# Graph layer with counted tiles: one-hot tiles handed over in runs of two or three, and tallies added two column groups late

## The chip, the cores and the metric

The kernel runs on one core of one Trainium2 chip. The metric is device time in microseconds (us) of one execution, the median of several runs; lower is better.

## What is computed

```python
def gnn(node_feats, src, dst, ...):
    neigh = segment_sum(node_feats[src], dst, num_segments=n)
    h = (1.0 + eps) * node_feats + neigh
    h = relu(h @ W1 + b1) @ W2 + b2
    return batch_norm(h) * gamma + beta

x = x + gnn(layernorm(x), src, dst, ...)          # 12500 nodes of 256 features, 200000 edges sorted by dst
x = x + ffn(layernorm(x), ...)                    # 8 experts, top 1, capacity 1.25
```

The edges are sorted by their target and are denser at low targets (the targets are 12500 times the square of a uniform number). The change lies wholly in the first step, `segment_sum(node_feats[src], dst)`.

## The kernel before

The program has four stages, one behind the other: `stage_norm` (layer norm, the table of rows in DRAM, and a plan of the edges), `stage_edges` (the segment sum and the two small matrix products), `stage_route` and `stage_experts`. Only `stage_edges` is touched.

An edge tile is 128 edges. The edges with the densest targets, 328 tiles (`HT`), are *counted*; all others, 1240 tiles, are *gathered*.

**Gathered tiles** come in 155 groups of 8 (`GT`), taken in iterations `n` of three groups `r` (`RG` = 3 buffers `got`). GpSimd (POOL) issues 8 indirect DMAs for each group (line 791). It may fill a buffer again once TensorE has finished the sums of the group that was in it (`s_sum`). VectorE makes 8 one-hot tiles `hot` for a group (L1070, L1076), TensorE multiplies them with the gathered rows, 16 matmuls (L879), and VectorE adds the result of the group before to the nodes (L1062).

**Counted tiles** are never gathered. For each, VectorE writes a wide one-hot of the source block (490 columns, L1113) and a one-hot of the target (128 columns, L1115) into a ring `tall` of `OR` = 6 tiles. TensorE multiplies the two (L907) into one of `BANKS` = 4 PSUM banks `tally`. Tiles that share a window of targets form a *column group* (`GROUP_OF`): 4 tiles for the first 96, 2 tiles up to tile 168, one tile each for the other 160, 220 column groups in all. When a column group is complete, VectorE adds its bank to `counts` (L1126, in `count(group)`). There are five units. After the tiles of a unit, `fold` adds what is still in the banks. Then for four iterations (mixed iterations) TensorE multiplies `counts` with pieces of the table (L917), which SP loads.

The order of work is written out and is the same on every engine, for each (n, r): the counted tiles of (n, r), then the gathered group, then pieces, then in some places a *quad*, the two matrix products of 512 nodes (L928, L936, L942 on TensorE; about 25 us in which TensorE does nothing else). 64 of the (n, r) have counted tiles, 3 to 12 each. Six quads stand directly ahead of an (n, r) with counted tiles: those at (13,1), (21,2), (28,2), (30,2), (36,0) and (38,0). Behind them come 4, 4, 3, 3, 5 and 3 tiles, all of one-tile column groups.

The handshake is one count per tile: TensorE waits for `s_tall >= t + 1` and signals `s_tile`; VectorE waits for `s_tile` before it writes a place of the ring again. With three column groups of delay, `counted(t)` at the start of column group g calls `count(g - 3)`.

Of the kernel before, what the change touches and what calls it, by code (L numbers as in the profile page):

```python
# [10 lines left out]
ALU = mybir.AluOpType  # L11
# [7 lines left out]
P = 128  # L19
# [18 lines left out]
RG = 3  # L38
# [4 lines left out]
GROUPS = ((96, 4), (168, 2), (328, 1))  # L43
NU = len(UNIT_TILES)
TW = 5
FIRST = tuple(sum(sum(tiles) for tiles in UNIT_TILES[:u]) for u in range(NU + 1))
HT = FIRST[NU]
PHASES = []
GROUP_OF = []
# [10 lines left out]
NIT = -(-NG // RG)  # L60
# [5 lines left out]
KEY = HI * TW  # L66
OH = KEY + P
# [19 lines left out]
TILES, MIXED = {}, {}  # L87
# [9 lines left out]
SPREAD = {n + 1: u for n, (u, i) in MIXED.items() if i == MIX - 1}  # L97
# [2 lines left out]
      18: (44, 1), 19: (45, 2), 1: (46, 1), 20: (47, 0), 21: (48, 1), 22: (49, 2), 23: (51, 0)}  # L100
ORDER = sorted(AT, key=lambda q: AT[q]) + [NQ - 1]
assert sorted(ORDER) == list(range(NQ)) and PIECES * RG * MIX * XK == HI - HI % XK


def closed_before(group):
# [196 lines left out]
def flat32(tensor):  # L302
    return tensor[:, :, :].rearrange("p a b -> p (a b)")
# [336 lines left out]
def stage_edges(nc, norm, halves, table, rows_of, targets, buf, ident, nodes, plan, stats, w1f, w2f, W1, W2, W1s, W2s, b1s,  # L640
                b2s):
    with ExitStack() as ctx:
# [3 lines left out]
        def psum(name, shape, dt):  # L646
            return ctx.enter_context(nc.psum_tensor(name, shape, dt))

        def sem(name):
            return ctx.enter_context(nc.semaphore(name))  # L650

        OR = 6
        BANKS = 4
# [3 lines left out]
        COUNT_ZEROS = -(-HI * CW // (2 * ZR * ROW))  # L657
        OWN = 17
        part = flat32(w1f).bitcast(F16)[:, 0:2 * XK * 2 * D].rearrange("p (r k d) -> p r k d", r=2, k=XK)
        tall = flat32(w2f).bitcast(F16)[:, 0:OR * OH].rearrange("p (r c) -> p r c", r=OR)  # L660
# [19 lines left out]
        tally = psum("e_tally", [P, BANKS, 2 * D], F32)  # L680
# [13 lines left out]
        s_tall, s_tile, s_count, s_fold, s_blank = (  # L694
            sem("e_tall_s"), sem("e_tile"), sem("e_count"), sem("e_fold"), sem("e_blank"))
# [22 lines left out]
        def quads_at(n, r):  # L718
            return [q for q in ORDER[:-1] if AT[q] == (n, r)]

        def tiles_at(n, r):

            tiles = TILES.get(n, ())
            parts = (0, 0, 1, 2) if n in SPREAD or n == 0 else (0, 1, 2, 3)
            return tiles[len(tiles) * parts[r] // parts[RG]:len(tiles) * parts[r + 1] // parts[RG]]

        def piece_number(u, i, r, c):
            return u * (MIX * RG * PIECES + 1) + (i * RG + r) * PIECES + c

# [4 lines left out]
        def pieces_at(n, r):  # L734
            if n not in MIXED:
                return []
            u, i = MIXED[n]
            last = i == MIX - 1 and r == RG - 1
            return [piece_number(u, i, r, c) for c in range(PIECES + last)]

        with nc.Block() as block:
# [102 lines left out]
            def _(pe):  # L844
# [5 lines left out]
                with pe.If(general_rounds(pe) > 0):  # L850
                    with pe.Fori(0, general_rounds(pe)) as g:
                        first, end_ = block_range(pe, pe.value_load(ranges_of[0:1, at(g)], min_val=0, max_val=1 << 14))
                        pe.wait_ge(s_pgot, g * (16 * PT) + 16 * PT)
                        with pe.Fori(first, end_):
# [3 lines left out]
                            for t in range(PT):  # L858
                                for half in range(2):
                                    ins = nc.tensor.matmul(sums[:, 0, 0:D], hot[:, 0, t, :],  # L860
                                                           some_rows[:, t, half * D:(half + 1) * D],
                                                           start=(t == 0 and half == 0), stop=(t == PT - 1 and half == 1))
# [2 lines left out]
                        pe.sem_inc(s_pfree, 1)  # L865
                    pe.reg_mov(turn, 1)

                pe.sem_inc(s_tile, OR)
                pe.sem_inc(s_used, 2)
                left = pe.alloc_register("left")  # L870

                def gathered_once(number):
                    r, place = number % RG, (number + 1) % 2
                    pe.wait_ge(s_got[r], (number // RG + 1) * (16 * GT))
                    pe.wait_ge(s_hot, number + 1)
                    pe.wait_ge(s_add, number + 1)
                    for t in range(GT):
                        for half in range(2):
                            ins = nc.tensor.matmul(sums[:, place, 0:D], hot[:, place, t, :],  # L879
                                                   got[:, r, t, half * D:(half + 1) * D],  # L880
                                                   start=(t == 0 and half == 0), stop=(t == GT - 1 and half == 1))
                    ins.then_inc(s_sum, 1)
# [17 lines left out]
                    pe.wait_ge(s_sum, turn)  # L900
                    pe.sem_inc(s_free, 1)

                def count(t):

                    group = GROUP_OF[t]
                    pe.wait_ge(s_tall, t + 1)
                    nc.tensor.matmul(tally[:, group % BANKS, 0:KEY], tall[:, t % OR, KEY:OH], tall[:, t % OR, 0:KEY],  # L907
                                     start=(t == GROUP_OF.index(group)), stop=(group not in GROUP_OF[t + 1:])
                                     ).then_inc(s_tile, 1)

                def piece(number):
                    k0, width = piece_columns(number)
# [34 lines left out]
                pe.wait_ge(s_w, 32)  # L947
                for n in range(NIT):
                    for r in range(RG):
                        for t in tiles_at(n, r):  # L950
                            count(t)
                        if n * RG + r < SINGLE:
                            gathered_once(n * RG + r)
                        elif n * RG + r < NG:
                            gathered(n, r)
                        for number in pieces_at(n, r):
                            piece(number)
                        for q in quads_at(n, r):
                            quad(q)
# [48 lines left out]
            def _(dve):  # L1008
# [99 lines left out]
                    ins.then_inc(s_spread, 1)  # L1108
                    dve.wait_ge(s_spread, flushed[0])

                def one_hots(t):
                    dve.wait_ge(s_tile, t + 1)
                    nc.vector.tensor_scalar(tall[:, t % OR, 0:KEY], plan.iota[:, :], plan.key[:, t:t + 1], None,  # L1113
                                            ALU.is_equal)
                    nc.vector.tensor_scalar(tall[:, t % OR, KEY:OH], plan.iota[:, 0:P], plan.low[:, t:t + 1], None,  # L1115
                                            ALU.is_equal).then_inc(s_tall, 1)

                def count(group):

                    last_tile = len(GROUP_OF) - 1 - GROUP_OF[::-1].index(group)  # L1120
                    column = dve.value_load(plan.cols[0:1, group:group + 1], min_val=0, max_val=P - 1)
                    dve.wait_ge(s_tile, OR + last_tile + 1)
                    if group > 0:
                        dve.wait_ge(s_count, group)
                    place = counts[:, :, bass.ds(column, TW)]
                    nc.vector.tensor_tensor(place, place, tally[:, group % BANKS, 0:KEY].rearrange("p (k d) -> p k d", d=TW),  # L1126
                                            ALU.add).then_inc(s_count, 1)

                def counted(t):

                    one_hots(t)
                    unit = max(u for u in range(NU) if FIRST[u] <= t)
                    if t == FIRST[unit] or GROUP_OF[t - 1] != GROUP_OF[t]:
                        group = GROUP_OF[t] - (BANKS - 1)
                        if group == GROUP_OF[FIRST[unit]]:
                            dve.wait_ge(s_blank, (unit + 1) * COUNT_ZEROS)
                        if group >= GROUP_OF[FIRST[unit]]:
                            count(group)

                def fold(u):  # L1140
                    for group in range(GROUP_OF[FIRST[u + 1] - 1] - (BANKS - 2), GROUP_OF[FIRST[u + 1] - 1] + 1):
                        count(group)
                    dve.wait_ge(s_count, GROUP_OF[FIRST[u + 1] - 1] + 1)
                    wide = counts[:, :, 0:CW - P]
                    nc.vector.tensor_tensor(wide, wide, counts[:, :, P:CW], ALU.add).then_inc(s_fold, 1)
# [19 lines left out]
                def quad(q, turns):  # L1165
                    k = ORDER.index(q)
                    if k > 0:
                        measure(ORDER[k - 1])
                    dve.wait_ge(s_add, turns)
                    nc.vector.tensor_scalar(hrow.rearrange("p t d -> p (t d)"), nodes[:, q, :], 1.0, None,  # L1170
                                            ALU.mult).then_inc(s_hrow, 1)

                for n in range(NIT):
                    if n in MIXED and MIXED[n][1] == 0:
                        fold(MIXED[n][0])
                    for r in range(RG):
                        for t in tiles_at(n, r):
                            counted(t)
                        if n * RG + r < SINGLE:
                            gathered_once(n * RG + r)  # L1180
                        elif n * RG + r < NG:
                            gathered(n, r)
                        if n in SPREAD and r == 0:
                            spread(SPREAD[n], n * RG + 2 if n * RG < SINGLE else turn)
                        for q in quads_at(n, r):
                            quad(q, n * RG + r + 2 if n * RG < SINGLE else turn)
# [820 lines left out]
```

## Time and profile before

| | |
|---|---|
| median of 3 runs | 3169.5 us |
| the runs | 3169.5, 3172.03, 3138.97 us |
| span of the profiled execution | 3175.1 us |
| busy in it: PE, PEld, DVE, ACT, POOL | 1826, 1098, 1443, 695, 1710 us |
| stage with the edges | from about 138 us to about 2290 us |
| counted tiles | from 141 us to 1700 us, in five stretches |

PE is TensorE's matmuls, PEld its weight loads, DVE VectorE, ACT ScalarE, POOL GpSimd; SP issues plain DMAs. The profile gives a span and no separate device time for the profiled execution; its span lies 5.6 us (0.2%) above the median. An idle time in a row is the time in which the engine had nothing to do just before the instruction, and the name behind the arrow is what ended it; "issue" means that the profile shows nothing it waited for, "remote" that the signal came from something that the profile does not place.

### The profile page before, as it was taken

The numbers are of one execution on the slowest core, as the hardware profiler recorded it, in microseconds if no ns is written. First come the engines' busy times: TensorE is split into PE (matmuls) and PEld (weight loads), VectorE is DVE, ScalarE is ACT, GpSimd is POOL, SyncE is SP. The second block draws the span as 40 slices with busy tenths as digits, with TensorE's granted clock in tenths as the row PEclk, the third lists the DMA queues.
The fourth block names the chain that finished last, engine by engine and source line by source line (L and its number), as shares of the span: only waits on it lengthen the run. The fifth ranks groups of instructions, "written<-read, shape, count | busy, mean of one in ns | idle before, by whom it ended". The sixth has DMA issues, their size and how long they took to land. (4 is left out here: it accounts for less than half of the span.)

```text
span 3175.1 us, 32785 instructions
## 1 busy us (share of the span) xinstructions
PE 1826.2 (58%) x9046; PEld 1097.7 (35%) x9047; DVE 1442.5 (45%) x4225; ACT 694.9 (22%) x1116; POOL 1710.4 (54%) x1690
## 2 busy tenths in 40 slices
PE   0154444455545455655554455564568768989995
PEld 0022212222222222322222222232357645566664
DVE  8765511543225422531252112122336557786885
ACT  6600000000010001000100001110046554636642
POOL 0366664655645565555644444445315556767874
PEclk9976667676767677777877777777776688999997
DMA  7533354324633354234423332212246432222220
GB/s 244 188 104 106 116 184 138 106 88 132 197 101 91 115 182 148 87 121 144 152 65 121 120 111 65 67 54 79 54 145 216 131 93 75 71 84 73 79 83 18
DMA packets 201521, 361.08 MB, mean 114 GB/s; under 512 B 62117, under 2 KB 125947, under 8 KB 201334
## 3 DMA queue, kind: packets, MB, share of 16 engines
q0 software_dynamic: 69152, 185.00, 19.3%
q1 hardware_dynamic: 130038, 172.60, 16.8%
q8 instruction: 108, 1.77, 0.2%
q10 hardware_dynamic: 2144, 1.05, 0.1%
q14 instruction: 79, 0.65, 0.1%
HBM read 291.08 MB, written 71.92 MB: 114 GB/s over the span
## 5 line engine op out<-in xcount | busy, mean ns | idle before, releaser
L791 POOL DMA_INDIRECT halves<-table,halves x1240 | 1187.7, 958 | 1011.5 <-issue 367.1
L879 PE MATMUL e_sums<-halves 128*128 128x256 f16 x1920 | 334.7, 346 | 392.8 <-issue 244.1
L1062 DVE SCALAR_TENSOR_TENSOR nodes<-e_sums,above,nodes 128x256 f32 (+1 forms) x161 | 77.3, 480 | 967.0 <-remote 437.4
L879 PEld LDWEIGHTS e_sums<-halves 128*128 128x128 f16 x1920 | 229.6, 122 | 508.3 <-issue 425.7
L936 PE MATMUL e_up<-e_hT,W1s 128*128 128x512 f32 (+1 forms) x400 | 229.8, 734 | 234.9 <-ACT e_hT L985 140.2
L985 ACT ACTIVATE e_hT<-e_up 128x1024 f32<-128x1024 f32 (+1 forms) x25 | 25.2, 1007 | 1524.0 <-remote 1185.3
L1720 POOL TENSOR_TENSOR x_midl<-x_midf,x_midh 128x512 f16<-128x512 f32 x200 | 298.7, 1517 | 104.9 <-ACT x_midh L1854 99.4
L917 PE MATMUL e_tally<-w1f,counts 128*128 128x512 f16 x490 | 165.5, 480 | 281.6 <-DMA w1f<-table 204.9
L1126 DVE TENSOR_TENSOR counts<-counts,e_tally 128x490 f32 x220 | 159.8, 726 | 267.8 <-PE e_tally L907 147.9
L1810 PE MATMUL x_down<-halves,x_midh 128*128 128x256 f16 x1472 | 249.4, 277 | 16.6 <-DVE x_yb L1947 15.0
L1786 PE MATMUL x_up<-x_xTh,halves 128*128 128x512 f16 (+1 forms) x800 | 233.6, 371 | 3.1 <-ACT x_midh L1854 3.1
L936 PEld LDWEIGHTS e_up<-e_hT,W1s 128*128 128x128 f32 x400 | 91.8, 240 | 355.8 <-issue 177.8
L1810 PE MATMUL x_down<-halves,x_midl 128*128 128x256 f16 x736 | 203.9, 277 | 0.0
L907 PE MATMUL e_tally<-w2f 128*128 128x490 f16 x328 | 126.0, 467 | 135.0 <-DVE w2f L1115 76.5
L1076 DVE TENSOR_SCALAR halves<-ring,e_rel 128x128 f16 x960 | 175.9, 273 | 59.0 <-issue 26.4
L942 PE MATMUL e_up<-e_mid,W2s 128*128 128x512 f32 (+1 forms) x400 | 183.8, 614 | 28.2 <-ACT e_mid L988 28.2
L917 PEld LDWEIGHTS e_tally<-w1f,counts 128*128 128x128 f16 x490 | 48.4, 113 | 374.6 <-DMA w1f<-table 235.4
L1734 POOL DMA_INDIRECT out<-x_res,x_nodei x100 | 116.1, 1161 | 87.3 <-issue 66.7
L1324 POOL DMA_INDIRECT slot_rows<-r_row,r_slots x100 | 97.7, 977 | 117.7 <-ACT r_row L1419 49.9
L1810 PEld LDWEIGHTS x_down<-halves,x_midh 128*128 128x128 f16 x1472 | 145.9, 99 | 40.4 <-issue 11.6
L1786 PE MATMUL x_up<-x_xTl,halves 128*128 128x512 f16 (+1 forms) x400 | 148.2, 371 | 0.0
L896 PE MATMUL e_sums<-halves 128*128 128x256 f16 x640 | 91.6, 305 | 89.5 <-DVE nodes L1062 55.6
(208 smaller groups left out, 2752.4 us busy)
## 6 DMA issues: line engine op xcount, KB each, us to landing
w1f<-table SPq DMA_DIRECT2D x120, 512.0 KB
halves<-table,halves POOLq DMA_INDIRECT x1240
slot_rows<-halves SPq DMA_DIRECT2D x64, 268.0 KB
x_row<-slot_rows SPq DMA_DIRECT2D x32, 536.0 KB, 7.4
table<-halves SPq DMA_DIRECT2D x25, 512.0 KB, 2.9
counts<-in_x SPq DMA_DIRECT2D x24, 512.0 KB, 4.5
r_xin<-in_x SPq DMA_DIRECT2D x24, 512.0 KB
out<-r_row SPq DMA_DIRECT2D x24, 512.0 KB
```

What stands on the lines that cost most here:

```text
L791: pool.indirect_dma_start(got[:, r, t, :], None, table.rearrange("p h d -> (p h) d"), bass.IndirectOffsetOnAxis(ap=idx[:, r, t:t + 1], axi ...
L879: ins = nc.tensor.matmul(sums[:, place, 0:D], hot[:, place, t, :], got[:, r, t, half * D:(half + 1) * D], start=(t == 0 and half == 0), st ...
L907: nc.tensor.matmul(tally[:, group % BANKS, 0:KEY], tall[:, t % OR, KEY:OH], tall[:, t % OR, 0:KEY], start=(t == GROUP_OF.index(group)), st ...
L917: ins = nc.tensor.matmul(product, counts[:, k0 + k, 0:P], part[:, number % 2, k, :], start=(k0 + k == 0), stop=(k0 + k == HI - 1))
L936: ins = nc.tensor.matmul(up[:, c % 2, 0:width], W1s[:, j, c * P:(c + 1) * P], hT[:, j, 0:width], start=(j == 0), stop=(j == DK - 1))
L942: ins = nc.tensor.matmul(up[:, c, 0:width], W2s[:, j, c * P:(c + 1) * P], mid[:, j, 0:width], start=(j == 0), stop=(j == H1C - 1))
L1076: ins = nc.vector.tensor_scalar(hot[:, place, t, :], plan.ring[:, ring_at(shift)], rel[:, place, t:t + 1], None, ALU.is_equal)
L1126: nc.vector.tensor_tensor(place, place, tally[:, group % BANKS, 0:KEY].rearrange("p (k d) -> p k d", d=TW), ALU.add).then_inc(s_count, 1)
L1720: nc.gpsimd.tensor_tensor(midl[:, j % 2, c, :], midf[:, c % MB, :], midh[:, j % 2, c, :], ALU.subtract).then_inc(s_mlo, 1)
L1734: pool.indirect_dma_start(out, bass.IndirectOffsetOnAxis(ap=nodei[:, j, t:t + 1], axis=0), res[:, j % RR, t, :], None, bounds_check=bound, ...
L1786: ins = nc.tensor.matmul(up[:, c % MB, 0:tiles * P], w[:, h, k, cols], x[:, j % 2, k, 0:tiles * P], start=(n == 0), stop=(n == len(passes) ...
L1810: ins = nc.tensor.matmul(down[:, t, :], m[:, j % 2, k, rows], w[:, h, k, :], start=(n == 0), stop=(n == len(passes) - 1))
```

## The change

- The tiles of an (n, r) are cut into runs: of three while the first tile is under 168, of two above, with a shorter run at the end where the number doesn't divide. 328 tiles give 149 runs (45 of three, 89 of two, 15 of one).
- VectorE writes all one-hots of a run and signals `s_tall` once; TensorE waits once, does the run's matmuls and signals `s_tile` once. VectorE waits before a run for the run that holds the tile 6 ahead of its last one.
- The tallies of column group g - 2 are added at the start of column group g, where it was g - 3. This happens after all one-hots of the run: `counted(run)` makes the run's one-hots first and then all adds that the run's tiles call for. `fold` is left with two adds where it had three.

```diff
+def runs_at(n, r):
+    tiles, runs = list(tiles_at(n, r)), []
+    while tiles:
+        size = 3 if tiles[0] < GROUPS[1][1 - 1] else 2
+        runs.append(tiles[:size])
+        tiles = tiles[size:]
+    return runs
+
+RUN_OF = [k for k, run in enumerate(run for n in range(NIT) for r in range(RG) for run in runs_at(n, r)) for _ in run]
...
-                pe.sem_inc(s_tile, OR)
...
-                def count(t):
-
-                    group = GROUP_OF[t]
-                    pe.wait_ge(s_tall, t + 1)
-                    nc.tensor.matmul(tally[:, group % BANKS, 0:KEY], tall[:, t % OR, KEY:OH], tall[:, t % OR, 0:KEY],
-                                     start=(t == GROUP_OF.index(group)), stop=(group not in GROUP_OF[t + 1:])
-                                     ).then_inc(s_tile, 1)
+                def count(run):
+
+                    pe.wait_ge(s_tall, RUN_OF[run[0]] + 1)
+                    for t in run:
+                        group = GROUP_OF[t]
+                        ins = nc.tensor.matmul(tally[:, group % BANKS, 0:KEY], tall[:, t % OR, KEY:OH],
+                                               tall[:, t % OR, 0:KEY], start=(t == GROUP_OF.index(group)),
+                                               stop=(group not in GROUP_OF[t + 1:]))
+                    ins.then_inc(s_tile, 1)
...
-                def one_hots(t):
-                    dve.wait_ge(s_tile, t + 1)
-                    nc.vector.tensor_scalar(tall[:, t % OR, 0:KEY], plan.iota[:, :], plan.key[:, t:t + 1], None,
-                                            ALU.is_equal)
-                    nc.vector.tensor_scalar(tall[:, t % OR, KEY:OH], plan.iota[:, 0:P], plan.low[:, t:t + 1], None,
-                                            ALU.is_equal).then_inc(s_tall, 1)
+                def one_hots(run):
+                    if run[-1] >= OR:
+                        dve.wait_ge(s_tile, RUN_OF[run[-1] - OR] + 1)
+                    for t in run:
+                        nc.vector.tensor_scalar(tall[:, t % OR, 0:KEY], plan.iota[:, :], plan.key[:, t:t + 1], None,
+                                                ALU.is_equal)
+                        ins = nc.vector.tensor_scalar(tall[:, t % OR, KEY:OH], plan.iota[:, 0:P], plan.low[:, t:t + 1],
+                                                      None, ALU.is_equal)
+                    ins.then_inc(s_tall, 1)
...
-                    dve.wait_ge(s_tile, OR + last_tile + 1)
+                    dve.wait_ge(s_tile, RUN_OF[last_tile] + 1)
...
-                def counted(t):
-
-                    one_hots(t)
-                    unit = max(u for u in range(NU) if FIRST[u] <= t)
-                    if t == FIRST[unit] or GROUP_OF[t - 1] != GROUP_OF[t]:
-                        group = GROUP_OF[t] - (BANKS - 1)
...
+                def counted(run):
+
+                    one_hots(run)
+                    unit = max(u for u in range(NU) if FIRST[u] <= run[0])
+                    for t in run:
+                        if t == FIRST[unit] or GROUP_OF[t - 1] != GROUP_OF[t]:
+                            group = GROUP_OF[t] - (BANKS - 2)
...
-                    for group in range(GROUP_OF[FIRST[u + 1] - 1] - (BANKS - 2), GROUP_OF[FIRST[u + 1] - 1] + 1):
+                    for group in range(GROUP_OF[FIRST[u + 1] - 1] - (BANKS - 3), GROUP_OF[FIRST[u + 1] - 1] + 1):
```

## Rows read from the trace of the kernel before

**Rows 1.** Busy time in stretches: all five counting stretches, then the rest.
```profile
138.00:382.00 244.00, 113.52 (x480) 57.43 (x480) 144.80 (x568) 0.00 (x0) 160.12 (x165) 0.70 0.36 109
534.00:741.00 207.00, 96.33 (x378) 50.54 (x377) 103.31 (x353) 11.91 (x20) 124.72 (x130) 0.69 0.37 112
880.00:1074.00 194.00, 94.00 (x345) 47.82 (x343) 85.83 (x285) 16.95 (x27) 101.42 (x108) 0.70 0.32 99
1231.00:1404.00 173.00, 89.46 (x322) 45.26 (x322) 79.62 (x265) 16.84 (x27) 96.57 (x101) 0.72 0.35 105
1555.00:1702.00 147.00, 74.53 (x266) 37.19 (x266) 63.00 (x208) 16.96 (x27) 71.95 (x77) 0.73 0.28 84
```

**Rows 2.** Timeline of POOL, 200 to 250 us: start, us, instruction, idle before.
```profile
201.14 0.99 POOL L791 DMA_INDIRECT halves<-table,halves  x1 [3.58 <-remote]
202.44 0.94 POOL L791 DMA_INDIRECT halves<-table,halves  x1 [0.30 <-issue]
...
224.87 1.00 POOL L791 DMA_INDIRECT halves<-table,halves  x1 [3.39 <-remote]
...
248.70 1.00 POOL L791 DMA_INDIRECT halves<-table,halves  x1 [3.53 <-remote]
```

**Rows 3.** What POOL waited for, 140 to 1702 us: us, times, longest.
```profile
POOL halves L791 <- issue: 277.8, 867, 2.0
POOL halves L791 <- PE e_sums L879: 192.1, 17, 25.3
POOL halves L791 <- remote: 137.5, 43, 5.4
POOL halves L791 <- DMA halves<-rows_of: 62.1, 6, 29.8
```

**Rows 4.** Timeline, counted tiles on VectorE with and without an add.
```profile
560.43 0.34 DVE L1113 TENSOR_SCALAR w2f<-iota,key 128x490 f16<-128x490 f16 x1
560.69 0.24 DVE L1115 TENSOR_SCALAR w2f<-iota,low 128x128 f16<-128x128 f16 x1
560.85 0.34 DVE L1113 TENSOR_SCALAR w2f<-iota,key 128x490 f16<-128x490 f16 x1
...
612.21 0.25 DVE L1115 TENSOR_SCALAR w2f<-iota,low 128x128 f16<-128x128 f16 x1
612.37 0.66 DVE L1126 TENSOR_TENSOR counts<-counts,e_tally 128x490 f32 x1
612.94 0.35 DVE L1113 TENSOR_SCALAR w2f<-iota,key 128x490 f16<-128x490 f16 x1
```

**Rows 5.** Timeline, the same engine's `hot` tiles, eight with one signal.
```profile
609.86 1.39 DVE L1076 TENSOR_SCALAR halves<-ring,e_rel 128x128 f16 x8 [0.26 <-issue]
```

**Rows 6.** Idle time ahead of line 1113 (VectorE), 140 to 1702 us.
```profile
L1113 DVE TENSOR_SCALAR w2f<-iota,key x328: 322/340/574, 141.3 to 1695.0; 128x490 f16<-128x490 f16 x164
  remote: 45.2, 6
  PE e_tally L907: 7.2, 2
```

**Rows 7.** Timeline behind the quad at (13,1), four tiles follow.
```profile
670.18 0.99 PE L907 MATMUL e_tally<-w2f 128*128 128x490 f16 x4
670.69 0.76 DVE L1126 TENSOR_TENSOR counts<-counts,e_tally 128x490 f32 x1 [24.84 <-PE e_tally L907]
671.33 0.21 DVE L1070 TENSOR_SCALAR e_rel<-cold,least 128x8 f32<-128x8 f32 x1
671.79 1.39 DVE L1076 TENSOR_SCALAR halves<-ring,e_rel 128x128 f16 x8 [0.26 <-DVE e_rel L1070]
673.29 1.95 PE L879 MATMUL e_sums<-halves 128*128 128x256 f16 x16 [2.12 <-issue]
676.06 1.10 POOL L791 DMA_INDIRECT halves<-table,halves  x1 [14.48 <-PE e_sums L879]
```

**Rows 8.** Timeline around the quad at (28,2), three tiles follow.
```profile
1280.30 1.39 DVE L1076 TENSOR_SCALAR halves<-ring,e_rel 128x128 f16 x8 [0.26 <-DVE e_rel L1070]
...
1304.44 0.79 PE L907 MATMUL e_tally<-w2f 128*128 128x490 f16 x3
1304.95 0.85 DVE L1126 TENSOR_TENSOR counts<-counts,e_tally 128x490 f32 x1 [22.06 <-PE e_tally L907]
1305.06 1.95 PE L879 MATMUL e_sums<-halves 128*128 128x256 f16 x16
1307.84 0.94 POOL L791 DMA_INDIRECT halves<-table,halves  x1 [16.57 <-PE e_sums L879]
```

**Rows 9.** Timeline, a group with four tiles at the lower clock.
```profile
603.45 3.57 PE L879 MATMUL e_sums<-halves 128*128 128x256 f16 x16 [7.29 <-issue]
603.65 0.48 DVE L1062 SCALAR_TENSOR_TENSOR nodes<-e_sums,above,nodes 128x256 f32 x1 [4.29 <-remote]
...
606.82 0.57 PE L907 MATMUL e_tally<-w2f 128*128 128x490 f16 x1
...
611.16 0.48 DVE L1062 SCALAR_TENSOR_TENSOR nodes<-e_sums,above,nodes 128x256 f32 x1
```

## What I predict, and how it follows

> **What bounds the kernel now.** I read four views in this order: busy time by stretch, the waits of POOL, the timeline of POOL, and the timeline of all engines around a counted group and around a quad.
>
> The change can act only where counted tiles are taken. Those are the five stretches of [rows 1], 244 + 207 + 194 + 173 + 147 = 965 us of the 3175. In none of them is an engine full: VectorE is busy 59% in the first (144.8 of 244) and 43% in the last, TensorE about half. POOL is the highest (160.1 of 244), and its 0.95 us per gather leaves out 0.30 us of issue between two gathers. With it a gather costs 1.25 us, a group of eight 10.0 us. Every sixteenth gather POOL also stands still for some 3.5 us: in [rows 2] the stops end at 201.14, 224.87 and 248.70, so sixteen gathers, two groups, take 23.8 us. The first stretch holds 165 gathers; 165 / 16 x 23.8 = 245 us, and it lasts 244. So in the first stretch, with 144 of the 328 tiles, POOL's own pace explains all of the time, and nothing that VectorE or TensorE do can be seen in it.
>
> In the other four stretches 416 gathers at this pace would take 619 us; they last 721. The 100 us on top are in [rows 3]: POOL waited 192 us for the sums of TensorE in 17 places from 140 to 1702 us. These are the quads: TensorE is taken for some 25 us, the three buffers are full, and POOL starts again when the first group behind the quad is summed. Six quads stand ahead of counted tiles. So two things set the end of this stage: POOL's pace, and after a quad the time from the quad's end to the end of the first sum. Only the second can be reached by the change.
>
> **The change, part by part.**
>
> *Signals and waits taken away.* 328 tiles become 149 runs, so 179 signals and 179 waits fall away on each of VectorE and TensorE. What did one cost? In [rows 4] the two one-hots of a tile start 0.26 us apart (560.43, 560.69), and the next tile's first, with signal and wait between, starts 0.16 us behind the second. The eight `hot` tiles of [rows 5], with no wait between them and the same 128 columns, take 1.39 us less some 0.25 for the last one's own length, over 7 steps: 0.16 us each. The same spacing with and without a handshake: it costs VectorE nothing. On TensorE the four matmuls behind a quad take 0.99 us [rows 7] and three take 0.79 [rows 8], so one costs 0.20 us, each with its own signal; 490 columns at 2.4 GHz are 0.20 us, so there is nothing to save there either. I take 0. The bounds: nothing below 0 is gained if the spacing tells all; if waits that were exposed go, at most the idle time ahead of line 1113, 52.4 us [rows 6].
>
> The Trainium skill speaks against this part too. "VectorE: DVE Perf Modes", section "The DRAIN you can't avoid", reports eight copies that took the same time with a semaphore after each and with one after the last. This case's trace agrees: 0.16 us either way. The page "TensorE: Matmul & The Clock Gate", section "The cost: per-tile semaphore tail", has the other view, about 26 ns for each increment of small packed tiles. By it, as an estimate, 179 fewer would save 4.7 us on TensorE; the rows leave no room for it between matmuls of 0.20 us.
>
> *TensorE starts a run later.* The first matmul of a run waits for the one-hots of its last tile: 0.42 us per further tile (560.43 to 560.85), so 0.42 or 0.84 us. TensorE is half idle, and what is behind it is the sum, which waits for the gather or for `hot`. `hot` is made after all counted one-hots, so it is later than the last run anyway. I take 0.
>
> *The adds come one column group earlier.* All 220 stay, with the same 0.57 us step (612.37 to 612.94 [rows 4]); VectorE's work is unchanged. What changes is what an add waits for. VectorE's queue is in order: one-hots of (n, r), adds, then `hot` of (n, r). An add that waits for a tile of the same (n, r) holds `hot` back until TensorE reaches that tile. Behind a quad TensorE reaches it only when the quad is over.
>
> - Before, with three tiles of one-tile column groups, the adds are g-3, g-2, g-1, all tiles of the group before; none waits. So `hot` was made at 1280.30, during the quad, and the sum started at 1305.06, 0.62 us after the first counted matmul (1304.44) [rows 8]. After, the runs are two and one, and the third tile calls for the add of the first. It waits for the quad to end. Then come: first matmul to add 0.51 us (670.18 to 670.69), 0.20 for the run's second matmul, the add 0.64 (to 671.33), the relative targets 0.46 (to 671.79), `hot` to the first sum 1.50 (to 673.29), all [rows 7]: 3.3 us. The sum starts 3.3 - 0.6 = 2.7 us later. Three quads are of this kind, (28,2), (30,2), (38,0): 8.1 us.
> - With four tiles, (13,1) and (21,2), one add waited before (670.69 [rows 7]); now the second run calls for two. That is one more add, 0.57 us, and the second matmul of the run, 0.20: 0.8 us. With five tiles, (36,0), it is the same: three adds behind the quad for two. Three quads: 2.4 us.
>
> Each is a delay of the first sum behind a quad, for which POOL is waiting (14.48 and 16.57 us idle, ended by the sum [rows 7, 8]), so it moves the stage one for one. Queued behind the held add are `hot`, the window add and the next one-hots. They are needed by the next sum, and POOL needs that one only 10 us later. Sum: 8.1 + 2.4 = 10.5 us.
>
> *Where POOL paces, the same wait is covered.* A group with counted tiles takes VectorE and TensorE 7.5 us from window add to window add (603.65 to 611.16 [rows 9], TensorE at the lower of its two levels, 1.2 GHz: the 16 matmuls take 3.57 us against 1.95 behind a quad). After the change it may take one add and one slow matmul more, 0.57 + 0.57 = 1.1 us: 8.6 us. POOL gives a group every 10.0 to 11.9 us. The cover is thin but holds. Without it the price would be 1.1 us in each of 64 groups.
>
> *Fold.* Two adds for three ahead of the fold, five times: at most 5 x 0.57 = 2.9 us earlier pieces. The third add has only moved ahead of `hot` of the group before. Pieces wait mostly for their loads. I take 0, and -2.9 for the lower end.
>
> *Total*: +10.5 us on the profiled span of 3175.1, 3185.6; on the median of the runs, 3169.5, that is 3180.
>
> **The rivals.**
>
> 1. *Nothing shows.* The delay behind a quad is given back: POOL's next stop for 3.5 us falls away or shifts when it has waited anyway. The stops are irregular after waits, which speaks for it; but they are 3.5 us and there are 43 of them, so they won't fit all six. Time 3169.5 or a few us on either side.
> 2. *Faster: exposed handshakes go.* If the stalls ahead of the one-hots come from the per-tile handshake and lie on the way to `hot`, all 52.4 us [rows 6] could go: 3169.5 - 52.4 = 3117. Against it: 45.2 of them are six stops of some 7.5 us, "remote", far too long for a missed handshake, and such stops end together with POOL's. It decides if more than 40 us of them lie where POOL is not the pace.
> 3. *Slower: the cover is too thin.* If the chain per group, not POOL, paces the counted groups after the change, 64 x 1.1 = 70 us: 3240. It needs the chain to grow from 7.5 to more than 10 us, so 2.5 us where I find 1.1; two low-clock matmuls and a missed ring place together could do it (a run waits for the whole run that holds the tile six back).
> 4. *A part of 3 behind the quads*: the two groups behind each of the six quads have their data already, so there the chain paces for a moment, 12 x 1.1 = 13 us more, 3193. I count it in the range of my forecast, since POOL needs only the first of these sums at once.
>
> **How the numbers follow.** Forecast (with 4) 0.52, rival 1 0.22, rival 2 0.14, rival 3 0.09, and 0.03 for something else. The runs shown spread from 3139 to 3172 without any change, 33 us, which is more than the effect. About 1%, 32 us, is what can be told from no change, so forecast and rival 1 are both "same". Own range of the forecast: 3169.5 - 2.9 to 3193 by the terms, and down to 3139 for the spread of runs. Towards rivals 2 and 3 I go half way down to 3117 and up to 3210, which leaves out most of each: 3137 to 3210. Faster 0.15, same 0.74, slower 0.11.
>
> **What would show it.** In the changed kernel: the first stretch still 244 us and POOL's sixteen gathers still 23.7 us; one-hots of a run 0.42 us per tile and no shorter; behind the quads at (28,2), (30,2) and (38,0) `hot` made after the quad, with the sum starting about 3.3 us after the first counted matmul instead of 0.6; behind (13,1) two adds between the first matmul and `hot`; POOL's waits for the sums larger by about 10 us in all. I am wrong if POOL's pace itself changes, if the idle time ahead of line 1113 disappears together with a shorter stage (rival 2), or if window adds in the first stretch come more than 11.9 us apart on average (rival 3).

## The result: slightly slower

The changed kernel takes 3171.2 us (median of 10 runs), the kernel before 3156.0 us in the same measurement (10 runs). The ratio is 1.0065, 95% interval 1.0036 to 1.0094: about 20 us more. The ratio leaves out runs more than 1.5% above the fastest run of their kernel, so it is not the quotient of the two medians, which lie 15.2 us apart. Measured again later, 12 runs beside 35 of the kernel before, the ratio was 1.0031 (1.0001 to 1.0060), about 10 us; I had expected 1.004 to 1.008 of this repetition. The forecast was +10.5 us (1.0033) and, with a chance of 0.74, a difference of under 1% either way.

The five counting stretches of the changed kernel, cut at the same iterations as [rows 1] (start and end, length, busy time and count of PE, PEld, DVE, ACT, POOL, granted clock, DMA share, GB/s):

```profile
138.00:382.00 244.00, 114.17 (x478) 57.37 (x479) 146.24 (x568) 0.00 (x0) 161.39 (x166) 0.68 0.37 110
520.00:729.00 209.00, 97.61 (x377) 50.13 (x378) 104.14 (x354) 11.91 (x20) 125.03 (x131) 0.67 0.37 112
872.00:1068.00 196.00, 94.80 (x334) 47.27 (x335) 86.47 (x283) 16.95 (x27) 99.31 (x105) 0.68 0.32 96
1232.00:1409.00 177.00, 92.57 (x320) 47.37 (x321) 80.34 (x263) 16.95 (x27) 94.29 (x99) 0.70 0.34 102
1552.50:1700.50 148.00, 77.97 (x264) 39.76 (x265) 63.30 (x207) 16.83 (x27) 76.16 (x80) 0.72 0.30 87
```

The first, which has no quad, is as long as before. The other four are 2, 2, 4 and 1 us longer. VectorE, ScalarE and POOL are as busy as before, within 4 us over all five: no work was added or saved. TensorE is busy 477 us, 9 us more than the 468 before, for the same matmuls: its granted clock is 0.01 to 0.02 lower in each stretch. What POOL waited for, 140 to 1702 us (us, times, longest), answers to [rows 3]:

```profile
POOL halves L806 <- issue: 270.6, 861, 2.0
POOL halves L806 <- PE e_sums L893: 211.2, 18, 25.4
POOL halves L806 <- remote: 140.9, 49, 5.1
POOL halves L806 <- DMA halves<-rows_of: 45.6, 5, 29.2
```

Its wait for the sums grew from 192.1 to 211.2 us. This is one execution of each, and the total moves by as much for other reasons (181.3 us in e3 below, which is as late behind the quads as the changed kernel), so the argument goes by the places themselves. The timeline behind the quad at (13,1), where four tiles follow, answers to [rows 7]:

```profile
655.97 0.99 PE L922 MATMUL e_tally<-w2f 128*128 128x490 f16 x4
656.69 0.75 DVE L1145 TENSOR_TENSOR counts<-counts,e_tally 128x490 f32 x1 [24.73 <-PE e_tally L922]
657.64 0.85 DVE L1145 TENSOR_TENSOR counts<-counts,e_tally 128x490 f32 x1 [0.21 <-DVE counts L1145]
658.37 0.21 DVE L1086 TENSOR_SCALAR e_rel<-cold,least 128x8 f32<-128x8 f32 x1
658.83 1.39 DVE L1092 TENSOR_SCALAR halves<-ring,e_rel 128x128 f16 x8 [0.26 <-DVE e_rel L1086]
660.33 2.83 PE L893 MATMUL e_sums<-halves 128*128 128x256 f16 x16 [3.36 <-issue]
663.98 0.98 POOL L806 DMA_INDIRECT halves<-table,halves  x1 [16.53 <-PE e_sums L893]
```

Two adds stand between TensorE's first counted matmul and the eight `hot` tiles, where there was one. The sum starts 4.36 us after that matmul, where it was 3.11. It also takes longer, 2.83 us instead of 1.95, and it is the sum's end that lets POOL go on: POOL's next gather comes 8.01 us after the first counted matmul (663.98), where it was 5.88 (676.06 [rows 7]). Before this sum TensorE had stood idle for 3.36 us, in the kernel before for 2.12. The granted clock (the figure ahead of the DMA share) during the sum is 0.65 in the changed kernel, first line, and 1.00 in the kernel before, second line:

```profile
660.30:663.20 2.90, 2.88 (x17) 2.17 (x18) 2.69 (x8) 0.00 (x0) 0.00 (x0) 0.65 0.00 0
673.30:675.20 1.90, 1.90 (x17) 1.55 (x17) 1.90 (x6) 0.00 (x0) 0.00 (x0) 1.00 0.00 0
```

And behind the quad at (28,2), three tiles, against [rows 8]:

```profile
1304.76 0.79 PE L922 MATMUL e_tally<-w2f 128*128 128x490 f16 x3
1305.48 0.85 DVE L1145 TENSOR_TENSOR counts<-counts,e_tally 128x490 f32 x1 [28.73 <-PE e_tally L922]
1306.20 0.21 DVE L1086 TENSOR_SCALAR e_rel<-cold,least 128x8 f32<-128x8 f32 x1
1306.66 1.39 DVE L1092 TENSOR_SCALAR halves<-ring,e_rel 128x128 f16 x8 [0.26 <-DVE e_rel L1086]
1308.16 1.95 PE L893 MATMUL e_sums<-halves 128*128 128x256 f16 x16 [2.62 <-issue]
1310.94 0.95 POOL L806 DMA_INDIRECT halves<-table,halves  x1 [23.54 <-PE e_sums L893]
```

`hot` is no longer made during the quad but after it: VectorE sat 28.73 us in front of the one add, and everything queued behind it sat with it. From the first counted matmul to the sum it takes 3.40 us instead of 0.62, and here the sum itself takes 1.95 us as before.

### The profile page after: what moved, and what is told of

The parts are those of the page before. It is cut to its first block and busy times, and to the rows that moved or that the text cites. A ratio compares the mean times of both kernels' runs of the same rounds, so it can differ in the third digit from the quotient of the medians.

```text
span 3178.2 us, 32784 instructions
## 1 busy us (share of the span) xinstructions
PE 1845.5 (58%) x9046; PEld 1115.1 (35%) x9047; DVE 1447.6 (46%) x4225; ACT 694.8 (22%) x1116; POOL 1708.0 (54%) x1690
## 3 DMA queue, kind: packets, MB, share of 16 engines
q10 hardware_dynamic: 2144, 1.05, 0.1%
## 5 line engine op out<-in xcount | busy, mean ns | idle before, releaser
L893 PE MATMUL e_sums<-halves 128*128 128x256 f16 x1920 | 350.3, 357 | 436.5 <-issue 279.0
L958 PE MATMUL e_up<-e_mid,W2s 128*128 128x512 f32 (+1 forms) x400 | 181.3, 607 | 20.2 <-ACT e_mid L1004 17.8
L910 PE MATMUL e_sums<-halves 128*128 128x256 f16 x640 | 90.1, 301 | 91.1 <-DVE nodes L1078 55.8
```

The source lines that it names most:

```text
L958: ins = nc.tensor.matmul(up[:, c, 0:width], W2s[:, j, c * P:(c + 1) * P], mid[:, j, 0:width], start=(j == 0), stop=(j == H1C - 1))
```

## The experiments

Theory A: the loss is made where VectorE's queue holds an add that waits for a tile of its own place, behind a quad, with the `hot` tiles behind it. Rival B: the runs cost, because TensorE starts later and VectorE waits for whole runs. Rival C: handshakes are worth something. Rival D: the lateness costs in all counted groups. Rival E: POOL gives back what it is delayed behind a quad.

In all experiments the adds are driven by one small function. A lag of L means that at the start of column group g all up to g - L are added:

```python
added = [0]

def adds(t, lag):
    unit = max(u for u in range(NU) if FIRST[u] <= t)
    first = GROUP_OF[FIRST[unit]]
    if t == FIRST[unit] or GROUP_OF[t - 1] != GROUP_OF[t]:
        while added[0] <= GROUP_OF[t] - lag:
            if added[0] == first:
                dve.wait_ge(s_blank, (unit + 1) * COUNT_ZEROS)
            count(added[0])
            added[0] += 1
```

`fold` adds what is left. `BEHIND_QUAD` is (13,2), (22,0), (29,0), (31,0), (36,1), (38,1). The ratios are to the kernel before on the same chip, with 12 runs of the experiment and 35 of before (10 and 10 in the row "changed"). The second column is the sum over the six places of the time from the first counted matmul behind the quad to the start of the sum, read from the timeline of each kernel as above; the third goes on to POOL's next gather, which starts 0.8 us after the sum's end. The profile is one execution of each kernel.

| kernel | to the sum, us | to POOL, us | median, us | before, us | ratio (95%) |
|---|---|---|---|---|---|
| before | 12.2 | 30.5 | | | 1 |
| changed | 23.8 | 45.0 | 3171.2 | 3156.0 | 1.0065 (1.0036 to 1.0094) |
| changed, again | 23.8 | 46.8 | 3143.9 | 3132.4 | 1.0031 (1.0001 to 1.0060) |
| e1: single tiles, lag 2 | 22.9 | 45.6 | 3157.5 | 3151.4 | 1.0038 (1.0001 to 1.0075) |
| e2: runs, lag 3 | 13.2 | 33.7 | 3151.1 | 3151.4 | 0.9989 (0.9955 to 1.0022) |
| e3: runs, lag 2, adds between | 24.1 | 45.4 | 3166.1 | 3151.4 | 1.0045 (1.0011 to 1.0080) |
| e4: lag 4 everywhere | 7.0 | 24.3 | 3172.3 | 3151.4 | 1.0090 (1.0056 to 1.0124) |
| e5: lag 2 in the six places only | 22.9 | 44.9 | 3152.9 | 3144.3 | 1.0017 (0.9982 to 1.0052) |
| e6: 3 us more in the six places | 20.8 | 42.3 | 3166.2 | 3144.3 | 1.0050 (1.0017 to 1.0082) |
| e7: 3 us more in 18 first groups | 12.2 | 31.6 | 3162.7 | 3144.3 | 1.0073 (1.0041 to 1.0104) |
| e8: lag 1 | 29.1 | 54.9 | 3146.7 | 3132.4 | 1.0055 (1.0028 to 1.0083) |
| e9: lag 4 in the six places only | 7.0 | 24.8 | 3144.2 | 3144.3 | 0.9998 (0.9963 to 1.0034) |
| f2: lag 2 everywhere but the six places | 12.2 | 31.8 | 3121.1 | 3132.4 | 0.9961 (0.9931 to 0.9991) |
| f4: lag 4, fold of three | 7.0 | 23.7 | 3132.5 | 3132.4 | 1.0017 (0.9983 to 1.0050) |

The lateness slows the sum too. In the changed kernel it starts 11.7 us later in all, and POOL goes on 14.5 us later (16.3 in the repetition); the rest is that three of the six sums took 2.58 to 3.27 us where they took 1.95 before. This is a tendency and no fixed toll: in f2 the sum behind (13,1) starts 3.11 us after the matmul as before and yet takes 3.44 us. But the third column less the second is 16.7 to 17.8 us in the kernels with lag 4 there, 18.3 to 20.5 in those with lag 3 (before, e2, e7, f2), and 21.2 to 25.9 in the delayed ones.

### Lateness without runs (e1)

```diff
-        size = 3 if tiles[0] < GROUPS[1][1 - 1] else 2
+        size = 1
...
+                    for k, t in enumerate(run):
+                        one_hots(run, k)
+                        adds(t, 2)
```

> One count per tile as before, but each tally is added two column groups late (as in the changed kernel) instead of three. Theory A (what costs is the lateness: an add waits behind a quad for a tile of the same place, and the one-hots for the gathered group with it): nearly the whole loss stays, ratio to before 1.002 to 1.006; behind the quads at (28,2), (30,2) and (38,0) the first sum starts 3 us or more after the first counted matmul, where it was 0.6. Rival B (the runs cost: TensorE starts a run later, VectorE waits for whole runs): ratio 0.999 to 1.001.

Ratio 1.0038, interval just above 1. Behind the quads with three tiles the sum starts 3.19, 3.11 and 3.12 us after the first counted matmul, as theory A says. There are no runs in this kernel, so the late `hot` is not their doing. The time by itself is weak against rival B: its 1.001 is inside the interval.

### Runs without lateness (e2)

```diff
+                    for k, t in enumerate(run):
+                        one_hots(run, k)
+                        adds(t, 3)
```

> Runs of two and three with one count each, as in the changed kernel, but each add is put between the one-hots of the run, behind its own tile, and is three column groups late as before. Theory A: the same as before, ratio 0.998 to 1.002, and the one-hots for the gathered group are made during the quad again where three tiles follow. Rival B: ratio 1.004 to 1.008, as the changed kernel. Rival C (handshakes are worth something): under 0.997.

Ratio 0.9989: no difference that can be measured. Behind the quad at (28,2), in its timeline:

```profile
1289.09 0.78 PE L922 MATMUL e_tally<-w2f 128*128 128x490 f16 x3
1289.71 1.95 PE L893 MATMUL e_sums<-halves 128*128 128x256 f16 x16
1289.80 0.85 DVE L1146 TENSOR_TENSOR counts<-counts,e_tally 128x490 f32 x1 [22.19 <-PE e_tally L922]
...
1292.49 0.94 POOL L806 DMA_INDIRECT halves<-table,halves  x1 [16.50 <-PE e_sums L893]
```

The sum is 0.62 us behind the first counted matmul, ahead of the add that VectorE waits with. The interval is -14 to +7 us. Rival B wanted 1.004 or more and is out. Rival C wanted under 0.997, and the interval reaches 0.9955: 179 handshakes fewer on each side bring nothing that shows, but a gain of a few us is not ruled out. The six places are 1.0 us longer to the sum than before and 3.2 to POOL, too little for the time to show.

### Adds between the one-hots (e3)

```diff
+                    for k, t in enumerate(run):
+                        one_hots(run, k)
+                        adds(t, 2)
```

with the runs of the changed kernel, which differs only in having the adds behind all one-hots.

> The changed kernel with one thing different: the adds stand between the one-hots of a run instead of all behind them. Two adds that follow each other directly start 1.06 us apart in the changed kernel's trace, adds with one-hots between them need only 0.57 us each. Theory A with the lateness alone: ratio to before 1.003 to 1.006. If the adds in a row carry a good part of the loss: 1.000 to 1.003.

1.0045, between the two measurements of the changed kernel. That two adds in a row cost more than two apart is seen in the trace (last section); in the time it is not seen.

### Six places only, and all but the six (e5, f2)

```diff
+                        adds(t, (2 if (n, r) in BEHIND_QUAD else 3))      # e5
...
+                        adds(t, (3 if (n, r) in BEHIND_QUAD else 2))      # f2
```

> The kernel before, one count per tile and adds three column groups late, but two late in the six places behind a quad alone: 25 of the 328 tiles (four, four, three, three, five and three of them, and what follows until the delay is three again). Theory A (the loss is made in these six places): about the same as with two late everywhere, ratio to before 1.002 to 1.005. Rival D (the loss is made in all counted groups, by more waits of VectorE for TensorE): 1.000, within the interval.

> The complement of the kernel that is two late in the six places alone: tallies two column groups late everywhere, three late in the six places behind a quad. One count per tile. Theory A: the first sum behind a quad starts 0.6 us after the first counted matmul again where three tiles follow, ratio to before 0.998 to 1.001. Rival D (the loss is made in all counted groups): 1.002 to 1.005.

e5 is at 1.0017, just under its expectation, and its interval (-6 to +16 us) holds both theory A's 11 us and nothing, so by itself it decides nothing. f2 tells more. It is two late in 58 of the 64 counted places and still 0.9961, under before, beyond its interval and below my expectation. So the lateness there, together with the fold of two adds that comes with it, costs nothing, and rival D has nothing to rest on but a gain at the fold that would hide a loss. Against e1, which differs in the six places alone, f2 is 0.0077 lower (the two intervals together: plus or minus 0.0048), 24 us with a margin of 15, where the timelines give 22.9 - 12.2 = 10.7 to the sum and 45.6 - 31.8 = 13.8 to POOL. The two were measured on different chips, each against the kernel before on its own; against the changed kernel measured again beside it, f2 is 0.0070 lower (plus or minus 0.0042). The middles of both are high: e5 leaves the six places at most 16 us.

The traces of all versions place the loss too. Take the time from a unit's first counted matmul to its first piece, which takes in the whole counting stretch and its fold. In the first unit, where no quad is, the six kernels that are one or two late in the ordinary groups (changed, its repetition, e1, e3, e8, f2) take 245.1 us on average (241.0 to 248.5), and the five that are three late and have nothing added there (before, e2, e5, e6, e9) take 244.2 (243.0 to 246.2). In the other four units together, the six that are late behind the quads (changed, its repetition, e1, e3, e5, e8) take 614.8 us (604.1 to 624.0), and before, e2, e7 and f2 take 604.3 (598.4 to 607.6). That is 10.5 us, give or take about 8. (e6, delayed there by its reductions, has 602.5 in its one execution.) In f2's trace the sum behind (28,2) comes at once:

```profile
1278.57 0.78 PE L923 MATMUL e_tally<-w2f 128*128 128x490 f16 x3
1279.08 0.85 DVE L1147 TENSOR_TENSOR counts<-counts,e_tally 128x490 f32 x1 [23.82 <-PE e_tally L923]
1279.19 1.95 PE L894 MATMUL e_sums<-halves 128*128 128x256 f16 x16
```

and POOL's wait for the sums, 140 to 1702 us, is low:

```profile
POOL halves L807 <- PE e_sums L894: 167.0, 22, 20.3
```

167.0 us against 192.1 [rows 3] and 211.2 in the changed kernel. The six places take no less than in the kernel before, so the 25 us under it are not theirs. f2 is also the one version that beats both kernels, by 11 us. Why it is under before, and not level with it, is not settled: its folds have two adds instead of three, which I had priced at 2.9 us at most. Among a dozen comparisons at 95%, one that lies just beyond its interval can also be chance.

### A larger dose (e8)

```diff
+                        adds(t, 1)
```

> One count per tile, tallies added one column group late: a larger dose. Every add waits for the tile just before it. Theory A with the six places alone: behind each quad one more add than with two late, some 0.9 us, 5 us over the kernel with two late (whose ratio was 1.004), 1.005 to 1.007. If waits in all counted groups cost too (rival D), clearly more, over 1.010.

1.0055, at the lower end of theory A's 1.005 to 1.007 and not over 1.010. Every add now waits for the tile before it, in all 64 places, and still no more is lost than the six places explain: 29.1 - 12.2 = 17 us to the sum and 24 us to POOL by the timelines, 17 us (9 to 26) by the ratio.

### A known delay in the six places (e6)

```diff
+                        if (n, r) in BEHIND_QUAD:
+                            for _ in range(5):
+                                nc.vector.tensor_reduce(spare[:, spared[0]:spared[0] + 1], plan.iota[:, :], AX.X, ALU.max)
+                                spared[0] += 1
```

> The kernel before with five reductions of 490 columns added on VectorE (about 0.6 us each, 3 us together) ahead of the one-hots of the gathered group, in the six places behind a quad alone. Measures how much of a delay there reaches the end. Where three tiles follow (three places) the reductions run during the quad and are hidden; where four or five follow they stand behind the add that waits for the quad. Theory A: one for one where it is not hidden, 3 x 3 = 9 us, ratio 1.003. Rival E (delays behind a quad are given back by POOL): 1.000.

The reductions are work that nothing reads. Behind (13,1):

```profile
656.17 0.76 DVE L1148 TENSOR_TENSOR counts<-counts,e_tally 128x490 f32 x1 [21.89 <-PE e_tally L924]
656.82 2.93 DVE L1211 TENSOR_REDUCE e_spare<-iota 128x1 f32<-128x490 f16 x5
```

The sum comes 5.97 us after the first counted matmul (before 3.11); where three tiles follow it stays at 0.62, the reductions being done during the quad. The six places grow by 8.6 us to the sum and 11.8 us to POOL, the time by 16 us (5 to 26). Rival E is out: a delay behind a quad reaches the end. One for one lies in the interval; how exactly it holds, a margin of 10 us can't say.

### The same delay where POOL paces (e7)

```diff
+                        if 0 < n < MIX + 3:
```

with the same five reductions.

> The kernel before with the same 3 us of VectorE work in all 18 groups of iterations 1 to 6, in the first stretch, where POOL paces (11.9 us for a group, the chain of VectorE and TensorE takes about 7.5). 54 us of work are added. Theory A: it is covered, first stretch still 244 to 247 us, ratio 0.999 to 1.002. Rival (the chain has little cover): up to 54 us more, 1.017.

1.0073: of 54 us added, 23 us (13 to 33) reach the end. I had expected none. In its trace POOL stands still in another rhythm. Its stops from 200 to 250 us:

```profile
199.56 1.00 POOL L807 DMA_INDIRECT halves<-table,halves  x1 [3.17 <-remote]
...
211.80 1.00 POOL L807 DMA_INDIRECT halves<-table,halves  x1 [2.14 <-remote]
...
224.01 1.00 POOL L807 DMA_INDIRECT halves<-table,halves  x1 [2.15 <-remote]
...
236.17 1.00 POOL L807 DMA_INDIRECT halves<-table,halves  x1 [2.05 <-remote]
```

One stop of 2.1 us per group instead of one of 3.5 per two groups [rows 2]: 12.2 us per group instead of 11.9. So the stops aren't a fixed toll after sixteen gathers as I had read them; they answer to how VectorE and TensorE stand. Over 18 groups this gives 18 x 0.3 = 5 us. From the stretch's first counted matmul to its first piece the trace has 254.3 us against 243.4 before, so 11 us of the 23 are lost in the stretch where the work was added. Where the rest goes this profile does not show: it is one execution, at 3155 us.

### More lag (e9, e4, f4)

```diff
+                    for k, t in enumerate(run):
+                        adds(t, 4)                        # e4; single tiles
+                        one_hots(run, k)
...
+                        if (n, r) not in BEHIND_QUAD:     # e9, behind the one-hots, beside the adds(t, 4) ahead
+                            adds(t, 3)
...
+                        if t + 1 in FIRST:                # f4, behind the one-hots
+                            adds(t, 3)
```

> The kernel before with the delay raised to four column groups (adds ahead of the tile's own one-hots) in the six places behind a quad alone, three everywhere else and at the folds. No add waits behind a quad where three or four tiles follow. With four late everywhere the time was 0.9% above before, which theory A did not expect. If that loss comes from the folds, which had four adds in a row, this kernel is at 0.996 to 1.000, about 5 us under before. If it comes from the adds ahead of the one-hots behind the quads, it stays above 1.003.

> The kernel before with the tallies added four column groups late, ahead of the tile's own one-hots (the bank that the tile needs is just free then), fold left with four. Theory A: behind five of the six quads no add waits any more; where four tiles follow the first sum starts about 0.9 us after the first counted matmul instead of 3.1, so 2.2 us less in two places and 0.6 in one: some 5 us less than before, ratio 0.997 to 1.000. Rival (lateness is not what costs): 1.000, or above if the fourth add ahead of the fold costs.

> Tallies four column groups late, ahead of the tile's own one-hots, everywhere (that kernel was at 1.009), but with one add drawn forward behind the last tile of each unit, so that the fold has three adds as before. If the long fold was what cost: 0.997 to 1.002. If it is the adds ahead of the one-hots in all groups: 1.006 to 1.010 still.

In all three the six places do what theory A says: behind (13,1) the sum starts 0.82 us after the first counted matmul (e9), and the six together take 7.0 us, 5 less than before.

```profile
657.60 0.99 PE L923 MATMUL e_tally<-w2f 128*128 128x490 f16 x4
658.11 0.77 DVE L1147 TENSOR_TENSOR counts<-counts,e_tally 128x490 f32 x1 [17.93 <-PE e_tally L923]
658.42 1.95 PE L894 MATMUL e_sums<-halves 128*128 128x256 f16 x16
```

The time does not follow. e9 is at 0.9998 (-12 to +11 us), too wide to see 5 us. e4 missed its expectation widely: 1.0090, as slow as the changed kernel or slower. f4, with one add moved from each fold, is at 1.0017, 0.0073 lower (plus or minus 0.0048, on another chip, each against its own kernel before). So the long fold is the likely cost in e4, and f2's short fold points the same way, but neither shows it by itself, and f4 is not faster than before although its six places are. Five folds with one add more, about 1 us each, would make 5 us, and 23 were lost. What a longer fold sets off is open. In the profiles of these kernels the fold's distance to the last counted tile and to the first piece varies by several us from fold to fold, more than the add, so they don't tell.

## Why the prediction was right, step by step

- **Handshakes cost nothing**: right as far as it can be seen. The spacing of one-hots in the changed kernel is the same, 0.42 us per tile within a run and across two, the busy time on VectorE too (1447.6 us against 1442.5), and e2, with the runs alone, is level. Rival 2 is out with it: of its 52.4 us of idle time ahead of the one-hots, 50.8 are still there. The page that speaks against this part of the change, "VectorE: DVE Perf Modes" in the Trainium skill ("The DRAIN you can't avoid"), is borne out by e2 as far as its interval goes.
- **A run starts TensorE later, at no cost**: right, by e2 again.
- **The six places**: right in kind and nearly in size. I had 2.7 us for three places and 0.8 for three, 10.5 in all. The timelines give 2.78, 2.69 and 2.69 us for the first kind and 1.25, 1.13 and 1.12 for the second, 11.7 in all. The step that was mis-sized is the second add: it was taken at 0.57 us, the step of an add with one-hots behind it, and takes 0.95 (656.69 to 657.64) behind another add. And one term was left out: I ended the count at the sum's start, though POOL waits for its end. With the slower sums (1.95 us before, up to 3.27 in places where it was 1.95) the six places cost POOL 14.5 us and not 10.5.
- **One for one to the end**: not contradicted, and not measured sharply. Counted to POOL's next gather, e6 lost 16 us (5 to 26) for 11.8, e8 17 us (9 to 26) for 24, f2 against e1 24 us (margin 15) for 13.8. The changed kernel lost 20 us (11 to 30) and 10 us (0 to 19) for 14.5 and 16.3. All intervals hold one for one. No run holds TensorE's granted clock fixed, so what the lateness costs by the wait and what by the slower sums is told apart in the timelines alone.
- **Covered where POOL paces**: right for this change and for a weaker reason than I gave. The first stretch is 244 us before and after, by VectorE's first instruction for iteration 7, and to its first piece 246.2 us against 243.4, within what kernels without the lateness take (243.0 to 246.2). But e7 shows that the cover is not whole: VectorE work of 3 us per group came through by four tenths. My reading of POOL's stops as its own fixed pace was wrong. Rival 3, 70 us, is out by the time. That it is so because the change adds waits but hardly any VectorE work to these groups (144.8 us busy in the first stretch, 146.2 after) is argued and not shown.
- **The second group behind a quad (rival 4)**: it hardly shows. Its sum ends 23.6 us later over the six places, but POOL needs it only 10 us after it goes on, and in five of the six places it is done by then.
- **Fold at 0**: open. e4 against f4, and f2, hint that an add at the fold is worth more than its own time.
- **The number itself owes something to luck.** 3180 us was worked out from a median of three runs, 3169.5, which stands at 3156.0 with ten; the base was 13.5 us too high and the loss, by the first ratio, 10 us too low. The stated range, 3137 to 3210, holds nearly every outcome short of rivals 2 and 3. Single executions of the kernel before spread from 3105 to 3180 us over the chips used, and 12 runs against 35 leave a margin of about 10 us, as large as the effect. What carries the mechanism is the timelines of the six places, read to a tenth of a us, with e2 and f2 beside e1.

## What to carry to other kernels

When a wait is moved from one instruction to another on an in-order engine, look at what is queued behind it at the places where the other engine is away for long. Here one add, moved one place forward, turned work that was done during a 25 us stretch of matmuls into work done after it, in six places out of 64; everywhere else no cost of the same move shows. Count such a delay to the instruction that the next engine waits for, here the end of the sum: TensorE, idle for longer, did that sum more slowly in three of the six places. And a handshake between two engines that both have room brought nothing that shows when it was coarsened (e2): price it first by comparing the spacing of instructions with and without one.

## What the hardware showed that I had not expected

Two adds into `counts` directly behind each other start 0.95 us apart (656.69, 657.64; 0.85 to 1.05 in the whole trace), with one-hots between them an add takes a step of 0.57 us [rows 4]. The kernel makes each add wait for the one before (`s_count`), and the second then stands idle for 0.21 us after the first has ended. The changed kernel has this in 51 places, the rows of the adds say (idle time of VectorE ahead of them, by what ended it):

```profile
  PE e_tally L922: 162.2, 20
  remote: 130.6, 25
  issue: 28.8, 35
  DVE counts L1145: 10.7, 51
```

With one-hots in between, as in [rows 4], no such idle time shows. The other surprise is POOL's stops: one of about 3.5 us after every 16 gathers in the kernel before, one of about 2.1 us after about every 8 when VectorE has 3 us more to do per group (e7). The changed kernel has two short ones as well, 1.7 and 2.4 us, early in its first stretch. What the stops are stays open. And the same 16 matmuls of a sum took 1.95 us behind 2.12 us of idle time of TensorE and 2.83 us behind 3.36, at granted clocks of 1.00 and 0.65.
